# A state-space layer's input pass: the normed rows turned by VectorE and transfers instead of TensorE

## The reference

```
ada = silu(c) @ Wada.T + bada
shift, scale, gate = split(ada, 3, axis=1)
x_ssm = ln(x, norm1_g, norm1_b) * (1 + scale) + shift
skip = x_ssm
x_ssm = ln(x_ssm, norm2_g, norm2_b)
mz = x_ssm @ Wz.T + bz
act_mx = silu(x_ssm @ Wx.T + bx)
# two scans over the 512 positions, forward and backward, of
# z = mz @ Wc.T + bc, with dlt, B, C = split(z @ Wdbc.T)
out = (act_mx * z1 + act_mx * z2) @ Wf.T + bf + skip
return x + gate * out
```

## Time and profile before

| | |
|---|---|
| runs, median (lowest to highest) | 5685.93 us (5684.82 to 5686.73) |
| the profiled execution | 5681.6 us |
| its span | 5679.5 us |
| input pass within the span | 2592 to 2909 us, 317 us |
| TensorE (PE) busy over the span | 5410.8 us, 95% |
| VectorE (DVE) | 4209.2 us, 74% |
| ScalarE (ACT) | 2919.1 us, 51% |
| GpSimd (POOL) | 2906.6 us, 51% |
| granted TensorE clock, mean | 0.989 |

### The profile page before, as it was taken

How to read it: one execution, slowest core, us unless ns; L and a number is a source line. 1 busy time by engine, 2 the same in 40 slices (tenths; PEclk the granted TensorE clock), 3 DMA queues, 4 the chain that set the end, 5 groups by cost and what they waited for, 6 DMA issues and landing times. The chain is left out here.

```text
span 5679.5 us, 136465 instructions
## 1 busy us (share of the span) xinstructions
PE 5410.8 (95%) x58478; PEld 3262.1 (57%) x58478; DVE 4209.2 (74%) x5904; ACT 2919.1 (51%) x4944; POOL 2906.6 (51%) x956
## 2 busy tenths in 40 slices
PE   8999989998999999978989999999999999999998
PEld 3555545554455555544445566666666666666665
DVE  1456545554466666673349999999999999999996
ACT  0122212222455555551247776777777677677774
POOL 0000000000000000003449999999999999999997
PEclk9999999999999999998999999999999999999999
DMA  6200021001000000004431111112111121201211
GB/s 237 80 34 33 32 71 34 31 29 65 11 1 20 17 21 17 21 20 164 167 120 50 52 34 62 65 60 69 54 43 55 60 67 54 73 24 62 65 59 33
DMA packets 146330, 321.90 MB, mean 57 GB/s; under 512 B 27721, under 2 KB 28362, under 8 KB 135514
## 3 DMA queue, kind: packets, MB, share of 16 engines
q1 hardware_dynamic: 142866, 308.25, 16.1%
q10 hardware_dynamic: 2896, 5.34, 0.3%
HBM read 238.66 MB, written 74.89 MB: 55 GB/s over the span
## 5 line engine op out<-in xcount | busy, mean ns | idle before, releaser
L2070 POOL TENSOR_TENSOR sc_state<-sc_state,sc_c_rows 128x2048 f32<-128x2048 f32 x512 | 2330.2, 4564 | 122.8 <-DVE sc_state L2381 121.4
L2381 DVE TENSOR_TENSOR_SCAN sc_state<-sc_decay,wide 128x512 f32<-128x512 f32 x2048 | 2335.2, 1198 | 28.0 <-PE wide L2240 20.8
L2240 PEld LDWEIGHTS wide<-sc_diag,sc_du_t 64*64 64x64 f32 x32768 | 1048.0, 133 | 527.0 <-issue 344.0
L2240 PE MATMUL wide<-sc_diag,sc_du_t 64*64 64x128 f32 x32768 | 1218.9, 272 | 19.9 <-DVE sc_state L2381 19.7
L2256 PE MATMUL wide<-sc_state,half 64*64 64x512 f32 x8192 | 1199.5, 592 | 7.5 <-POOL sc_state L2070 7.0
L2174 ACT ACTIVATE sc_decay<-sc_delta,neg_a 128x512 f32<-128x512 f32 x1024 | 723.6, 719 | 448.7 <-DVE sc_state L2381 443.6
L2174 ACT ACTIVATE sc_decay<-sc_delta_x,neg_a 128x512 f32<-128x512 f32 x1024 | 710.1, 717 | 286.7 <-DVE sc_state L2381 282.5
L2256 PEld LDWEIGHTS wide<-sc_state,half 64*64 64x64 f32 x8192 | 405.8, 133 | 168.6 <-issue 127.5
L1491 DVE CUSTOM_DVE_ANT_0 l_prob<-wide,l_mask_add 128x512 f32<-128x512 f32 x512 | 339.6, 682 | 211.6 <-PE wide L1323 211.4
L1232 ACT ACTIVATE l_prob<-l_prob,l_s_max 128x512 f32<-128x512 f32 x512 | 366.0, 716 | 250.4 <-DVE l_s_max L1491 250.4
L2213 PE MATMUL wide<-set 128*128 128x512 f32 x1024 | 476.2, 608 | 0.0
(11 more groups left out here) (244 smaller groups left out, 6912.6 us busy)
## 6 DMA issues: line engine op xcount, KB each, us to landing
sc_c_rows<-c_d SPq DMA_DIRECT2D x64, 1024.0 KB, 4.8
set<-wz_tiles SPq DMA_DIRECT2D x128, 256.0 KB, 2.7
x<-ahead_out SPq DMA_DIRECT2D x24, 1024.0 KB, 4.8
ahead_x_wk<-x SPq DMA_DIRECT2D x16, 1024.0 KB, 5.7
sc_mx<-mx_d SPq DMA_DIRECT2D x64, 256.0 KB, 2.7
mx_d<-fr_mx SPq DMA_DIRECT2D x14, 1024.0 KB, 4.4
pro_wc<-in_wcT SPq DMA_DIRECT2D x4, 2048.0 KB, 19.2
xn_d<-fr_xn_t SPq DMA_DIRECT2D x8, 1024.0 KB, 4.2
```

Of the source, the lines that this page charges most:

```text
L2070: pool.tensor_tensor(state[quad % STATES][:, :, :], state[quad % STATES][:, :, :], c_rows[(r * 4 + q) % ROWS][:, :, :], ALU.mult).then_inc ...
L2240: last = pe.matmul(to[cols_to, k, :, :], du_t[slot % 2][rows, k, of * 64:(of + 1) * 64], diag[r % 2][rows, c, k, :, :], start=True, stop=True)
L2381: dve.tensor_tensor_scan(state[quad % STATES][:, step % 4, order], decay[step % DECAYS][:, order], pair[:, i, order], 0.0, ALU.mult, ALU.a ...
```

## The change

Row 0 is turned as before. For rows 1 to 7 three steps stand in place of the transposes:

1. VectorE turns `xn` right behind L1864, in four instructions of 128x512. Each turns every block of 32x32 within itself and writes the blocks to a new tile, `turned`. Then a block has its right inner order, but lies on the wrong group of 32 partitions.
2. SP moves the blocks to their partitions: sixteen transfers from SBUF to SBUF, one for each pair of groups, of 32 partitions x 2 KB in runs of 512 bytes, 64 KB each. They go into `xn`, whose old content is read by then. They stand behind the b_d store and ahead of the mx_d stores.
3. ScalarE applies scale and bias with four instructions, now from SBUF, into `xn_t`. They stand behind the seventh mx tile of the row before (m == 6) and ahead of the eighth.

TensorE goes straight from the last mx tile of a row to the L1778 matmuls of the next, and waits there for the four tiles of `xn_t`.

```
+        turned = sb("turned", [P, 4, DT, TT, 32])
 # SP
+                def move_blocks(b):
+                    sp.wait_ge(blocks_turned, b * TT)
+                    for i in range(4):
+                        for k4 in range(4):
+                            sp.dma_start(xn[b % 2][k4 * 32:(k4 + 1) * 32, :, i * P:(i + 1) * P],
+                                         turned[i * 32:(i + 1) * 32, k4, :, :, :].rearrange("c k t r -> c k (t r)")
+                                         ).then_inc(blocks_moved, 16)
...
                     sp.dma_start(d["b_d"][b].rearrange("(t p) n -> p t n", p=P),
                                  b_tm[:, :, :, :].rearrange("p t s n -> p t (s n)")).then_inc(b_stored, 16)
+                    if b + 1 < B:
+                        move_blocks(b + 1)
 # ScalarE
+                def scaled(b):
+                    act.wait_ge(blocks_moved, b * 256)
+                    if b >= 2:
+                        act.wait_ge(xn_stored, (b - 1) * 16)
+                    for k in range(DT):
+                        act.activation(xn_t[b % 2][:, k, :].rearrange("p (t i r) -> p t i r", t=TT, i=4),
+                                       xn[b % 2][:, k, :].rearrange("p (i t r) -> p t i r", t=TT, i=4), ACT.Identity,
+                                       scale=cols[:, G2 + k:G2 + k + 1], bias=cols[:, B2 + k:B2 + k + 1]
+                                       ).then_inc(t_drained, 1)
...
+                        if m == 6 and b + 1 < B:
+                            scaled(b + 1)
 # TensorE
-                    for k in range(DT):
-                        if k == 0:
-                            pe.wait_ge(xn_ready, (b + 1) * TT)
-                        if b * DT + k >= 2:
-                            pe.wait_ge(t_drained, b * DT + k - 1)
-                        for t in range(TT):
-                            last = pe.transpose(banks[k % 2][:, t * P:(t + 1) * P], xn[j][:, t, k * P:(k + 1) * P],
-                                                ident[:, :])
-                        last.then_inc(t_full, 1)
+                    if b == 0:
+                        pe.wait_ge(xn_ready, TT)
...
                     pe.wait_ge(t_drained, (b + 1) * DT)
 # VectorE
                     for t in range(TT):
                         dve.tensor_scalar(xn[j][:, t, :], xs[j][:, t, :], mv2[:, t, 0:1], rstd2[:, t:t + 1],
                                           ALU.subtract, ALU.mult).then_inc(xn_ready, 1)
+                    if b >= 2:
+                        dve.wait_ge(blocks_moved, (b - 1) * 256)
+                    for t in range(TT):
+                        dve.wait_ge(xn_ready, b * TT + t + 1)
+                        dve.transpose(turned[:, :, :, t, :].rearrange("p j k r -> p k j r"), xn[j][:, t, :]
+                                      ).then_inc(blocks_turned, 1)
```

More of the change, by code:

```diff
@@ L1610, in front_layer @@
         dlt_stored, b_stored, c_stored = sem("dlt_stored"), sem("b_stored"), sem("c_stored")
+        blocks_turned, blocks_moved = sem("blocks_turned"), sem("blocks_moved")
         with nc.Block() as block:
@@ L1729, in c_rows @@
                     act.activation(c_t[:, :], banks[3][0:2 * N, :], ACT.Copy).then_inc(c_ready, 1)
-                for b in range(B):
-                    for k in range(DT):
[L1733 to L1737, removed]
+                def scaled(b):
[7 more added lines that the diff above has]
+                                       ).then_inc(t_drained, 1)
+                for k in range(DT):
+                    act.wait_ge(t_full, k + 1)
+                    act.activation(xn_t[0][:, k, :], banks[k % 2], ACT.Identity, scale=cols[:, G2 + k:G2 + k + 1],
+                                   bias=cols[:, B2 + k:B2 + k + 1]).then_inc(t_drained, 1)
+                for b in range(B):
                     for m in range(ET):
@@ L1762, in _ @@
                     j = b % 2
-                    for k in range(DT):
-                        if k == 0:
-                            pe.wait_ge(xn_ready, (b + 1) * TT)
-                        if b * DT + k >= 2:
-                            pe.wait_ge(t_drained, b * DT + k - 1)
-                        for t in range(TT):
-                            last = pe.transpose(banks[k % 2][:, t * P:(t + 1) * P], xn[j][:, t, k * P:(k + 1) * P],
-                                                ident[:, :])
-                        last.then_inc(t_full, 1)
+                    if b == 0:
+                        pe.wait_ge(xn_ready, TT)
+                        for k in range(DT):
+                            if k >= 2:
+                                pe.wait_ge(t_drained, k - 1)
+                            for t in range(TT):
+                                last = pe.transpose(banks[k % 2][:, t * P:(t + 1) * P], xn[0][:, t, k * P:(k + 1) * P],
+                                                    ident[:, :])
+                            last.then_inc(t_full, 1)
                     pe.wait_ge(t_drained, (b + 1) * DT)
@@ L1860, in _ @@
                     dve.wait_ge(rstd2_ready, b + 1)
-                    if b >= 2:
-                        dve.wait_ge(t_full, (b - 1) * DT)
+                    if b == 2:
+                        dve.wait_ge(t_full, DT)
+                    if b >= 3:
+                        dve.wait_ge(t_drained, (b - 1) * DT)
                     for t in range(TT):
```

## The result

The changed kernel takes 5719.85 us, the median of five runs (5715.8 to 5721.22), against 5685.93 of before: 1.0056 times as long, 95% interval 1.0042 to 1.0070. The forecast was 5704 in a range of 5676 to 5736: the direction and the mechanism held, the loss is 34 us instead of 18. The time lies above the 5696 to 5713 that the forecast named as its own and next to the low end of rival C, 5721. The profiled execution took 5715.8 us with a span of 5713.7.

What follows compares the result with a forecast made beforehand. TensorE was taken to bound the input pass. Periods 4.5, row 1 3.4 and clock 10.2 summed to +18.1 us on 5681.6, 5699.7; the median's 4.3 us more gave 5704, range 5676 to 5736.

Steps and rivals of the forecast that it cites:

- rival C: Rival, chance 0.24: moves 0.64 us apart and landing late, or turns at 1.4 us; chain 42 to 45 us, time 5721 to 5742.
- the periods: Six row periods, row 1 to row 7, each 0.75 us longer than the old 38.82: +4.5 us.
- the clock: Low clock at the head of each of seven rows, 1.7 us each, less the one of before: +10.2 us.
- row 1: First changed row, counted apart: xn ready at 2626.11, then 15.7 us of chain, 2641.8 against 2638.39: +3.4 us.
- The head of the chain: VectorE writes the next row's xn only after drains(b), which waits for c_turn: ready 23.87 us into TensorE's row.
- The turns: Four turns of 128x512 on VectorE: 2.5 us, bounds 1.91 and 5.6.
- The issues: Sixteen transfers issued on SP, fifteen spacings of 0.54 us: 8.1 us, bounds 5.4 and 9.6.
- Landing: Last transfer's time from issue to landing: 1.7 us, bounds 1.4 and 2.7.
- activations: Four activations on ScalarE from SBUF: 3.1 us, bounds 2.8 and 3.4.
- Cover: Delay to VectorE's queued statistics costs nothing; the eighth mx activation and SP work behind it are covered for some 5 us.
- Rival B: Rival, chance 0.14: SP issues 0.36 us apart, chain 36.9 us, clock left as it was; -11 us, 5675.
- A2: Rival, chance 0.17: the same chain, but TensorE's clock stays high but for one row; +7.9 us, 5694.

## Why the prediction was right, and where its sizes were off

The mechanism is the one forecast: TensorE waits for a chain that is longer than its own row, and the wait brings the low clock. Three sizes were too small, all in the same direction, so no error hid another: the periods by 9.3 us, the clock by 5.9, row 1 by 1.7. Together with the 1.73 us that row 0 began sooner they lead from the 18.1 of the forecast to the 33.2 of the profile.

- **The head of the chain, 23.87 us.** Right: in the row at 2685.20 xn is ready at 2711.89, which is 26.69 us, less the 2.82 that the slow block cost. That this head decides is shown by the run that moved it: the same work, issued as slowly, fits.
- **The turns, 2.5 us.** They took 2.4.
- **The issues, 8.1 us.** This is the term of the chain that was mis-sized: 9.68 us, 0.645 per issue. My 0.54 leant on b_d and mx_d, stores to HBM, and 0.64 was only my upper bound. The runs show that these sixteen cost more because they write to SBUF and not to HBM (0.63 against 0.465), that runs of 512 or 2048 bytes change it by 0.02 us, and that 32 or 128 partitions don't change it. What makes it so stays open.
- **Landing 1.7, activations 3.1, hand-overs 0.3.** 2.12, 2.93 and under 0.1. Sum of the chain 41.07, forecast 39.57. So the periods cost 13.8 us where I had 4.5.
- **The clock, 1.7 us per row in all seven rows.** In all seven rows, yes, but at 2.54 us each: 16.1 more than before instead of 10.2. The rule of the Trainium skill that waits for data throttle TensorE ("TensorE: Matmul & The Clock Gate", section on HAM oscillation) agrees with this trace, 7 of 7 after 5.9 us. I took the size from blocks that were slow after 0.87 and 3.25 us. After 5.9 us and more the clock granted over the block was 0.54 to 0.71, against 0.68 in the block of 5.40 us in the kernel before, so in six of seven the stretch at 1.2 GHz reaches further into the block, in four nearly to its end (0.54 to 0.57).
- **Row 1, +3.4.** It was 5.1: from xn to the first L1802 matmul it is 17.4 us where I had 15.7, and the issues account for that.
- **Cover.** The work queued behind the turns and behind the four activations cost nothing: VectorE still waits 10.15 us for GpSimd ahead of xs, and ScalarE waits 13 us for TensorE at the first mx tile. Rival B needed issues at 0.36 and never had them; A2 needed a clock that holds.
- **Rival C.** Of the cases with a price, its low end came nearest: 5721 for moves at 0.64 and a late landing. The moves were at 0.645, and the landing was 2.1 us instead of 1.7. The reason that C gave for a late landing, that small transfers use only part of the DMA engines, finds no support: the landing over 128 partitions was 1.9 us, and their issues were no quicker. So the time came to lie in the range by its upper part, which C had put there, and not by the forecast's own.

## What to carry to other kernels

Work taken off the bounding engine is worth only what the new chain leaves of it: place the chain's head first (here a wait for a bank two steps away, which had cost nothing before), then count its issues. A wait that opens on TensorE can be paid twice: here 5.9 us of standstill were followed by 2.5 us more in a slow block, where 1.4 us were followed by none. The same change was a loss of 34 us with its head behind that wait and a gain of 23 us with its head ahead of it and row 1 left alone.

## What the runs showed of the hardware that I had not expected

- One DMA issue of 64 KB in a burst on SP took 0.63 to 0.645 us from SBUF to SBUF, whether of 32 or 128 partitions, in runs of 512 or 2048 bytes, and 0.465 us from SBUF to HBM. With SP and ScalarE issuing side by side it was 0.65 us on SP and 0.66 to 0.75 on ScalarE. Why the writes to SBUF are dearer no run shows; loads from HBM into SBUF were 0.64 us apart with 64 partitions, and 0.64 or 0.47 with 128.
- How long TensorE stood and what the dlt block behind it took: 0.16 us, 3.70 in twelve rows of twelve (the two runs with the early head); 1.4 us, 3.70 in six of six (two queues); 2.8 to 3.3 us, 5.40 in two of six and else 3.70 (the run to HBM, rows 2 to 7); 2.93, 3.97 and 4.38 us, 6.67, 6.35 and 6.07 (row 1 of the runs with two queues, with six matmuls and to HBM); 5.9 to 7.7 us, 5.2 to 6.8 in all seven of the changed kernel. The length of the standstill alone doesn't tell: 2.93 us were followed by 6.67, and 3.34 us by 3.70.
- VectorE turned 128x512 float32 in blocks of 32x32 at 0.68 us an instruction, four in 2.48 us, no dearer than an addition of that shape.
